# A new order of work in the second stage, on all four compute engines

## The chip, the core and the metric

One core of a Trainium2 chip runs the whole kernel. The metric is device time in microseconds of that core; lower is better. The core has TensorE (PE: matmuls and turns, into eight banks of PSUM), VectorE (DVE), ScalarE (ACT), GpSimd (POOL) and SyncE (SP, which issues the DMAs). Each runs its own list of instructions in order, and they wait for each other on semaphores.

## The reference

Two layers work on x of 4 sequences x 512 tokens x 128 features. The first layer and the attention of the second are not touched. What matters here is the feed-forward part of the second layer, a stack of six (`DEPTH`) local transformers:

```python
for i in range(6):
    x = attn_layer(shift_tokens(x), Wqkv[i], q_scale[i], k_scale[i], Wo[i]) + x
    x = ffn_layer(shift_tokens(x), ln_g[i], ln_b[i], W1[i], b1[i], W2[i], b2[i]) + x
# attn_layer: qkv = x @ Wqkv (128 -> 3 x 1024); q, k, v: 16 heads of 64
#   q = l2norm(q) * q_scale;  k = l2norm(k) * k_scale;  rotary tables on both
#   softmax of 8 * q k' over windows of 32 queries x 64 keys;  out = (attn @ v) @ Wo
# ffn_layer: hg = layernorm(x) @ W1 + b1 (128 -> 2 x 341);  a, gate = split(hg)
#   (a * gelu(gate)) @ W2 + b2
# shift_tokens: the upper half of the features comes from the token before
```

## The kernel before

The stack is cut into batches (a layer and one of its 4 sequences: 24 in all) and each batch into four tiles of 128 tokens. A tile is worked on in three consecutive slots. In slot g the projections and rotations of tile g are made, tile g-1 has its queries and keys turned and its scores and first softmax part made, and tile g-2 gets its exponentials, values and output turn. `t` is the position of a slot in its batch, 0 to 3; I call them slot 0 to slot 3. `run_slots` (L401) calls one `slot` function per engine, and each of these is a list of calls written out by hand: this list alone sets the order on its engine. No planner is involved.

What a slot holds, by the names used below:

- TensorE: six projections of 128 x 512, each three matmuls (`project`, L950): Q0, Q1, K0, K1, V0, V1 (c = 0 to 5), alternately into the two banks of `pj`; the turn of the queries and that of the keys (`turn`, L962, four 128 x 128 turns into each bank of `tr`); the turn of the probabilities (`turn_probs`) and of the outputs (`turn_out`), also in `tr`; the scores in two halves into `sc` (`window_scores`, 64 small matmuls each) and the values in two halves into `oo` (`values`).
- VectorE: for each of Q0, Q1, K0, K1 a rotation (`rotate`, L1580: two products, one with the cosine and one with the sine table) and a length sum (`lengths`); two clamps; the first softmax part (`soft1`: maximum and subtraction), the sums of the exponentials (`soft2`), and the weighting of the outputs (`weighted`).
- ScalarE: a square of each of Q0 to K1 (`square`; the rotation waits for it and the next projection in that bank for the rotation), the exponentials, six copies out of `tr` before and two after (`take_qk_part`, `take_probs`, `take_out`), the mask written into `sc`, two copies of V (`copy_v`), and two inverse roots (`inverse_root`, L1959: Ln, then Exp).
- POOL: adds the two products of a rotation (L2141), refines the inverse root in four small steps, and scales the rotated rows (L2155), once for the queries and once for the keys. `low_half` makes the small parts of the input rows.
- SP: eight or ten DMAs that lay the values out by windows (`windows`), and at a change of layer the new weights.

Beside this some slots hold work of the batches before (fillers). With m1 the batch before and m2 the one before that: slot 0 has the up projection of m2 in three chunks (`ff_up`), with `gelu` on ScalarE and `ff_gate` on VectorE; slot 1 the down projection (`ff_down`); slot 2 half 1 of the output projection of m1 (`wo_half`), then its norm: shifted input, entry turn (`norm_in`), statistics; slot 3 the norm's apply, return turn (`norm_back`) and end (`ln_finish`), and at its end half 0 of the output projection of the batch itself.

At a change of layer ScalarE rounds each new weight matrix to its high part (`weights_high`) and VectorE or POOL makes the low part (`weights_low`), K0, K1, V0 and V1 of the next layer wait for theirs. `log_exp_tables` (L1765) writes out a load of ScalarE's tables that serve Ln and Exp. Other loads are put in by the compiler where a function needs one; they show at the line of the activation (L1761).

Of the kernel before, what the change touches and what calls it, by code (L numbers as in the profile page):

```python
# [11 lines left out]
ALU = mybir.AluOpType  # L12
# [96 lines left out]
def build(nc, ins, out):  # L109
    ctx = ExitStack()  # L110
    with ctx:
# [251 lines left out]
        FFB = (sc, tr, oo)  # L363
        LD_W = (ld_q, ld_k, ld_v)
        LNB_BANKS = (oo[:, 0], oo[:, 1])
# [186 lines left out]
        def _(pe):  # L552
# [470 lines left out]
            def slot(s_):  # L1023
# [3 lines left out]
                tiles = g - 2 if new or b == 0 and t < 3 else NTILE  # L1027

                def values_(i):
                    if i == 0 and t == 0 and m1 is not None:  # L1030
                        pe.wait_ge(lnb_out, m1)
                        pe.wait_ge(y_att, m1 * 2 + 1)
                    if i == 0 and t == 1 and m2 is not None:
                        pe.wait_ge(ff_ev, m2 * FFC + 3)
                    if i == 0 and t == 3 and m1 is not None:
                        pe.wait_ge(lnb_norm, m1 + 1)
                    values(n2, g - 2, t2, i)

                def turn_probs_():
                    pe.wait_ge(e_exp, g - 1)  # L1040
                    for j in range(2):
                        if c_:
                            pe.wait_ge(qk_cp, g * 4 - 4 + j + 1)
                        else:
                            pe.wait_ge(o_cp, g * 2 - 6 + j + 1)
                        turn_probs(g - 2, j)

                def turn_q():
                    for j in range(2):
                        if g == 2:  # L1050
                            pe.wait_ge(qk_cp, 2 + j + 1)
                        wait(pe, o_cp, g * 2 - 6 + j + 1)
                        turn(g - 1, t - 1, j)

                def turn_k():
                    for j in range(2):
                        if d_:
                            pe.wait_ge(pt_cp, g * 2 - 4 + j + 1)
                        else:
                            pe.wait_ge(qk_cp, g * 4 - 4 + j + 1)  # L1060
                        turn(g - 1, t - 1, 2 + j)

                def out_():
                    for j in range(2):
                        if c_:
                            pe.wait_ge(qk_cp, g * 4 - 4 + 2 + j + 1)
                        else:
                            pe.wait_ge(pt_cp, g * 2 - 4 + j + 1)
                        if t == 0 and m2 is not None:
                            pe.wait_ge(ff_ev, m2 * FFC + 2)  # L1070
                        if t == 1 and j == 1 and m2 is not None:
                            pe.wait_ge(y_ff, m2 + 2)
                        turn_out(g - 2, j)

                def wo_half(m, i):
                    pe.wait_ge(o_cp, (m * T + 2 + 2 * i) * 2)
                    half = slice(i * (S // 2), (i + 1) * (S // 2))
                    for p_ in range(PAIRS):
                        last = mm((oo, sc)[i][:, 0, half], wo[:, p_, :], oT[:, p_, half], start=(p_ == 0),
                                  stop=(p_ == PAIRS - 1))  # L1080
                    if i == 1:
                        last = mm(sc[:, 0, 0:S // 2], w_hi[0][:, 0:P], xs_hi[:, 0:S // 2], start=False,
# [3 lines left out]
                def ff_down(m):  # L1086
                    for k, (o, w) in enumerate(CH):
                        pe.wait_ge(ff_ev, m * FFC + 3)
                        last = mm(tr[:, 1], w2[0:w, k, :], fa[0:w, k, :], start=(k == 0), stop=(k == FFC - 1))
                    last.then_inc(w2_mm, 1)  # L1090

                def value_part(c):
                    if new:
                        if b == 0 and t == 0 and c == 4:
                            pe.wait_ge(wl_ok[2], l + 1)
                        project(g, t, c)

                if new:
                    if b == 0 and t == 0:
                        pe.wait_ge(wl_ok[0], l + 1)  # L1100
                    if t < 2:
                        pe.wait_ge(xs_l, n * 2 + t + 1)
                    project(g, t, 0)
                    project(g, t, 1)
                if c_:
                    turn_q()
# [1112 lines left out]
```

## Time and profile before

| | |
|---|---|
| median of 3 runs | 2330.42 us (2330.19 to 2330.95) |
| the profiled execution | 2331.1 us, its span 2329.3 us |
| PE / DVE / ACT / POOL busy | 2055.0 / 1827.6 / 1499.3 / 1164.6 us |
| granted clock of TensorE, mean | 0.979; 1.00 in nearly all of the second stage |
| second stage (six layers) | from about 620 us to the end |

Busy shares are of the span. Matmuls overlap each other in the trace, so busy TensorE isn't TensorE at its peak; the start of one instruction to the start of the next is what it occupies.

### The profile page before, as it was taken

To read this page: it belongs to the slowest core of one execution; us is meant where nothing else is said; L and a number is where in the kernel's file an instruction comes from. 1 tells how busy PE (TensorE), PEld (TensorE's weight loads), DVE (VectorE), ACT (ScalarE), POOL (GpSimd) and SP (SyncE) were. 2 spreads that over 40 slices of the span, in tenths; PEclk is the share of its full clock that TensorE was granted. 3 is DMA by queue.
4 is the path that set the end of the run, shared out by engine and by line. 5 is a ranking of instruction groups with operands and counts; after the bars stand their busy time and mean duration, and the time that the engine had idled before them with its cause. 6 is when DMAs were issued, how large, how long until landed. Compare 5 with 4: busy or idle time off the path is not lost.

```text
span 2329.3 us, 82692 instructions
## 1 busy us (share of the span) xinstructions
PE 2055.0 (88%) x34492; PEld 1472.0 (63%) x34492; DVE 1827.6 (78%) x3797; ACT 1499.3 (64%) x2993; POOL 1164.6 (50%) x1373
## 2 busy tenths in 40 slices
PE   6888899887589999999999998999989999989996
PEld 4656654455367766667667666766666766666763
DVE  6778764578589888888887888888887888888883
ACT  4666653365266677676777667666676666767663
POOL 1111100000377666666666666666676666766660
PEclk9999999999699999999999999999999999999998
DMA  4000000000122222222322223322222322322221
GB/s 107 2 1 2 2 1 1 0 1 1 51 76 64 70 74 73 72 64 57 99 64 70 66 55 84 81 63 69 58 82 65 82 55 71 90 59 66 70 59 33
DMA packets 94677, 125.84 MB, mean 54 GB/s; under 512 B 27484, under 2 KB 42466, under 8 KB 94306
## 3 DMA queue, kind: packets, MB, share of 16 engines
q1 hardware_dynamic: 94306, 120.54, 19.7%
q8 instruction: 276, 4.52, 0.8%
q14 instruction: 95, 0.78, 0.1%
HBM read 21.91 MB, written 1.05 MB: 10 GB/s over the span
## 4 chain that ended last, share of the span: by engine, by line
PE 46%; DVE 13%; ACT 12%; issue 8%; POOL 2%; DMA 1%; SPq 0%; ACTq 0%; POOLq 0%; DVEq 0%
PE pj L554 12%; PE oo L554 10%; PE sc L554 10%; ACT arena L1761 9%; PE tr L557 9%; PE tr L554 5%; DVE arena L1592 2%; DVE arena L1590 2%; DVE xn L1209 1%; DVE arena L1611 1%; DVE arena L1613 1%; PE oo L557 1%; DVE stats L1197 1%; DVE arena L1622 1%; DVE arena L1598 1%
## 5 line engine op out<-in xcount | busy, mean ns | idle before, releaser
L1761 ACT ACTIVATE arena<-tr 128x512 f32<-128x512 f32 (+2 forms) x874 | 456.3, 570 | 144.6 <-PE tr L557 96.5
L2141 POOL TENSOR_TENSOR arena<-arena 128x1024 f32<-128x1024 f32 x192 | 456.5, 2377 | 159.8 <-DVE arena L1592 153.1
L1761 ACT ACTIVATE arena<-pj 128x512 f32<-128x512 f32 x576 | 338.9, 592 | 271.0 <-PE pj L554 269.9
L557 PE MATMUL tr<-ident,arena 128*128 128x128 f32 x2974 | 426.0, 278 | 66.2 <-ACT arena L1761 45.0
L1761 ACT ACTIVATE arena<-arena 128x16 f32<-128x16 f32 (+6 forms) x808 | 354.5, 452 | 125.0 <-DVE arena L1606 69.1
L557 PEld LDWEIGHTS tr<-ident,arena 128*128 128x128 f32 x2974 | 340.8, 141 | 147.7 <-issue 105.8
L2155 POOL TENSOR_TENSOR arena<-arena 128x1024 f32<-128x1024 f32 x192 | 365.6, 1904 | 27.8 <-POOL arena L2151 0.4
L1590 DVE TENSOR_TENSOR arena<-pj,rtab 128x512 f32<-128x512 f32 x384 | 259.8, 677 | 116.6 <-ACT arena L1761 112.5
L1592 DVE TENSOR_TENSOR arena<-pj,rtab 128x512 f32<-128x512 f32 x384 | 261.5, 681 | 0.0
L2109 POOL TENSOR_TENSOR rstd<-rstd,half_neg 128x4 f32<-128x4 f32 x40 | 40.6, 1016 | 438.6 <-DVE rstd L1204 438.6
L1598 DVE TENSOR_REDUCE arena<-arena 128x8 f32<-128x512 f32 x384 | 259.7, 676 | 0.0
L554 PE MATMUL oo<-slab,arena 64*32 64x64 f32 (+1 forms) x12416 | 229.8, 228 | 27.5 <-DVE xn L1209 13.2
L554 PE MATMUL pj<-w_lo,xs_hi 128*128 128x512 f32 x576 | 228.5, 397 | 0.0
L554 PEld LDWEIGHTS oo<-slab,arena 64*32 64x32 f32 (+1 forms) x12416 | 157.8, 106 | 111.7 <-issue 78.1
L1611 DVE TENSOR_REDUCE arena<-sc 128x16 f32<-128x1024 f32 x96 | 117.6, 1225 | 117.2 <-PE sc L554 116.8
L554 PEld LDWEIGHTS sc<-arena 64*32 64x32 f32 x12288 | 135.1, 105 | 95.9 <-issue 94.0
L554 PE MATMUL sc<-arena 64*32 64x64 f32 x12288 | 168.7, 224 | 9.9 <-issue 8.3
L1631 DVE TENSOR_TENSOR slab<-oo,arena 128x1024 f32<-128x1024 f32 x96 | 117.0, 1219 | 11.5 <-PE oo L554 10.1
L1377 DVE CUSTOM_DVE_ANT_0 arena<-pj,biases 128x128 f32<-128x128 f32 (+3 forms) x214 | 101.0, 486 | 28.9 <-PE pj L554 28.1
L1613 DVE TENSOR_TENSOR arena<-sc,arena 128x1024 f32<-128x1024 f32 x96 | 117.5, 1224 | 3.3
L2145 POOL TENSOR_TENSOR arena<-arena 128x16 f32<-128x16 f32 x192 | 45.4, 236 | 144.8 <-ACT arena L1761 144.7
L1622 DVE TENSOR_REDUCE arena<-arena 128x16 f32<-128x1024 f32 x96 | 116.0, 1209 | 0.0
(275 smaller groups left out, 3800.5 us busy)
## 6 DMA issues: line engine op xcount, KB each, us to landing
slab<-arena SPq DMA_DIRECT2D x576, 128.0 KB
slab<-arena SPq DMA_DIRECT2D x336, 64.0 KB
wqkv<-in_L_ffn_Wqkv SPq DMA_DIRECT2D x18, 512.0 KB, 3.8
wo<-in_L_ffn_Wo SPq DMA_DIRECT2D x6, 512.0 KB, 4.3
w<-in_L_ffn_W SPq DMA_DIRECT2D x6, 341.0 KB
YT<-in_L_attn_x SPq DMA_DIRECT2D x4, 256.0 KB, 3.9
arena<-in_L_ffn_W SPq DMA_DIRECT2D x1, 1024.0 KB
out_x<-arena SPq DMA_DIRECT2D x4, 256.0 KB, 2.3
```

The lines of the kernel that those rows point to most:

```text
L554: return nc.tensor.matmul(o, l, r, start=start, stop=stop, **k)
L557: return nc.tensor.transpose(o, i, ident[0:i.shape[0], 0:i.shape[0]])
L1590: v.tensor_tensor(ra[:, t % 2, k, co].rearrange("p (h u d) -> p h u d", u=2, d=DL // 2), src, tc_.unsqueeze(1).broadcast_to(wide), ALU.mult)
L1592: v.tensor_tensor(rb[:, k, co].rearrange("p (h u d) -> p h u d", u=2, d=DL // 2), src[:, :, ::-1, :], ts_.unsqueeze(1).broadcast_to(wide), ...
L1598: v.tensor_reduce(ss[:, k, hf * PAIRS:(hf + 1) * PAIRS, 0], sq[:, c % 2].rearrange("p (h d) -> p h d", d=DL), AX.X, ALU.add).then_inc(ss_o ...
L1611: v.tensor_reduce(mx, s_v, AX.X, ALU.max).then_inc(mx_ok, 1)
L1613: v.tensor_tensor(Tm.rearrange("p (a u) b -> p u a b", u=2), sc[:, :, :].rearrange("p u (a b) -> p u a b", b=2 * WIN), mx.rearrange("p (u ...
L1622: v.tensor_reduce(sm, Ex, AX.X, ALU.add).then_inc(sm_ok, 1)
L1631: v.tensor_tensor(On.rearrange("p (a u d) -> p u a d", u=2, d=DL), oo[:, :, :].rearrange("p u (a d) -> p u a d", d=DL), ri.rearrange("p (a ...
L1761: return nc.scalar.activation(o, i, f, **k)
L2141: p_.tensor_tensor(r_, r_, rb[:, k, :], ALU.add).then_inc(sum_ok, 1)
L2155: p_.tensor_tensor(r3, r3, rs[:, k, :].unsqueeze(2).broadcast_to([P, HL, DL]), ALU.mult).then_inc(qk_rdy, 1)
```

## The change

All of it lies in the second stage. No matmul, activation or vector operation is added or taken away. The slot lists of TensorE, VectorE, ScalarE and POOL are written anew, the same for all four positions. In short:

- Half 0 of the output projection moves from the end of slot 3 to slot 0 of the next batch, ahead of K0, and into another bank; both halves and the down projection now stand between the query turn and K0.
- Chunk 0 of the up projection goes to `oo` in place of `sc`, the down projection to `oo` in place of `tr`, the norm's return turn to `tr` in place of `oo`.
- The query turn stands behind chunk 0 and half 1 of the output projection; the probabilities behind K0; V0 behind the second half of the values.
- VectorE does both query rotations before the length sums, and both key rotations before the third one.
- ScalarE: the inverse roots stand late in the slot, behind V's copies, and the first of them between the GELUs of chunks 0 and 1; the copies of outputs are the last of the slot. The mask stands behind the fourth square.
- POOL makes both additions first and scales later.
- The low part of the key weights is made at the start of the layer instead of at the end of the one before.

```diff
-        FFB = (sc, tr, oo)
+        FFB = (oo, tr, oo)
+        WOB = (sc[:, 0], oo[:, 1])
-        LNB_BANKS = (oo[:, 0], oo[:, 1])
+        LNB_BANKS = (oo[:, 0], tr[:, 0])
```

The new order on TensorE (what is not in a new place is left out):

```diff
+                    queries(0)
+                    queries(1)
                 if t == 0 and m2 is not None:
+                    wait(pe, on_ok, weighted_)
                     pe.wait_ge(lnb_out, m2 + 1)
...
                     ff_up(m2, 0)
                 if t == 2 and m1 is not None:
+                    wait(pe, on_ok, weighted_)
                     wo_half(m1, 1)
+                if c_:
+                    turn_q()
+                if t == 0 and m1 is not None:
...
+                    pe.wait_ge(t_sub, g - 1)
+                    wo_half(m1, 0)
+                if t == 1 and m2 is not None:
+                    ff_down(m2)
...
                     project(g, t, 2)
                 if d_:
+                    probs()
+                if new:
+                    project(g, t, 3)
+                if d_:
                     values_(0)
                 if c_:
                     turn_k()
-                if t in (2, 3) and d_:
+                if d_:
                     values_(1)
+                if t == 3 and m1 is not None:
+                    if c_:
+                        pe.wait_ge(qk_cp, (g - 1) * 4 + 3)
...
+                    norm_back(LNB, LNB_BANKS[1], m1)
                 if new:
...
+                    project(g, t, 4)
+                if c_:
+                    window_scores(g - 1, (t - 1) % T, 0)
                 if t == 0 and m2 is not None:
...
                     ff_up(m2, 1)
+                if t == 2 and m1 is not None:
...
+                    norm_in(LNB, LNB_BANKS[0], xsF)
+                if new:
+                    project(g, t, 5)
                 if t == 0 and m2 is not None:
...
+                    pe.wait_ge(ff_ev, m2 * FFC + 1)
                     ff_up(m2, 2)
                 if c_:
                     window_scores(g - 1, (t - 1) % T, 1)
-                if t == 0 and d_:
+                if d_:
                     out_()
```

Waits that the new banks bring: the values of slot 0 wait for gate 0, those of slot 1 for the feed-forward sum, those of slot 2 for the second attention sum; the output turn of slot 3 waits for the end of the norm.

VectorE's new order: R0, R1, L0, [slot 0: gate 0], [slot 3: norm apply], L1, [slot 0: attention sum 0], [slot 1: feed-forward sum], [slot 2: attention sum 1], `soft2`, R2, clamp 0, R3, L2, `weighted`, [last batch of a layer, slot 0: tables], L3, clamp 1, [slot 0: gates 1, 2], [slot 2: norm statistics], `soft1` (R rotation, L length sum). Before, each L followed its R, gate 0 stood ahead of `weighted`, and gate 2 and the norm statistics stood behind `soft1`.

ScalarE:

```diff
+                if new:
+                    wait(ac, ss_ok, g * 4 - 1)
+                    square(g, 0)
+                    wait(ac, ss_ok, g * 4)
+                    square(g, 1)
...
+                    act(Ex, Tm, ACT.Exp, scale=8.0).then_inc(e_exp, 1)
+                if c_:
+                    take_qk_part(g - 1, (t - 1) % T, 0)
+                if t == 0 and m2 is not None:
+                    gelu(m2, 0)
+                if c_:
+                    take_qk_part(g - 1, (t - 1) % T, 1)
+                if new:
+                    ac.wait_ge(ss_ok, g * 4 + 1)
+                    square(g, 2)
...
+                    take_probs(g2, 0)
...
+                    take_probs(g2, 1)
...
+                    square(g, 3)
+                if layer_end:
+                    weights_high(l + 1, 0)
+                if t == 2 and m1 is not None:
...
+                    shifted(xsF, YT[:, s_.y1:s_.y1 + S], 0, S).then_inc(xs_f, 1)
+                if c_:
...
+                    mask(g - 1, (t - 1) % T)
+                    take_qk_part(g - 1, (t - 1) % T, 2)
+                    take_qk_part(g - 1, (t - 1) % T, 3)
...
+                    copy_v(g, t, 0)
+                if layer_end:
+                    weights_high(l + 1, 1)
...
+                    ln_finish(LNB, LNB_BANKS[1], m1, lcur[:, 0:1], lcur[:, 1:2], hB)
+                if new:
+                    inverse_root(g, 0)
+                if t == 0 and m2 is not None:
+                    gelu(m2, 1)
+                if new:
+                    copy_v(g, t, 1)
+                if t == 0 and m2 is not None:
+                    gelu(m2, 2)
+                    log_exp_tables()
+                if new:
+                    inverse_root(g, 1)
+                if d_:
...
                         take_out(g2, t2, j)
```

POOL:

```diff
+                if s_.new:
+                    add_parts(g, t, 0)
+                    if s_.ahead is not None and b == B - 1 and t == T - 1:
+                        weights_low(l + 1, 0)
+                    add_parts(g, t, 1)
+                    newton(g, 0)
+                    if t == 0:
+                        low_half(n * 2 + 2, YT[:, s_.y0:s_.y0 + S], P, S)
+                    scaled(g, t, 0)
+                    if s_.ahead is not None and t == 1:
+                        low_half(n * 2 + 3, YT[:, s_.ahead:s_.ahead + S], 0, P)
+                    newton(g, 1)
+                if t == 2 and s_.m1 is not None:
                     power(LNB, s_.m1)
                 if s_.new:
...
+                    scaled(g, t, 1)
```

## Rows read from the trace of the kernel before

**Rows 1.** The page: busy time and share per engine; the chain by engine.
```profile
PE 2055.0 (88%) x34492; PEld 1472.0 (63%) x34492; DVE 1827.6 (78%) x3797; ACT 1499.3 (64%) x2993; POOL 1164.6 (50%) x1373
...
PE 46%; DVE 13%; ACT 12%; issue 8%; POOL 2%; DMA 1%; SPq 0%; ACTq 0%; POOLq 0%; DVEq 0%
```

**Rows 2.** Windows, slots 0 to 3: stretch, length, busy by engine, clock, DMA, GB/s.
```profile
1505.61:1523.49 17.88, 17.18 (x320) 11.62 (x319) 13.42 (x22) 13.85 (x23) 10.01 (x10) 1.00 0.19 51
1523.49:1539.56 16.07, 14.60 (x313) 10.35 (x312) 13.15 (x21) 10.79 (x24) 10.45 (x13) 1.00 0.33 91
1539.56:1555.30 15.74, 15.74 (x329) 12.89 (x328) 13.49 (x21) 11.26 (x23) 9.95 (x11) 1.00 0.27 71
1555.30:1573.89 18.59, 16.04 (x327) 12.50 (x326) 18.32 (x39) 11.77 (x24) 14.26 (x21) 1.00 0.27 68
sum 68.28, PE 63.56 PEld 47.36 DVE 58.38 ACT 47.67 POOL 44.66; mean PE 15.89 PEld 11.84 DVE 14.60 ACT 11.92 POOL 11.16
```

**Rows 3.** Timeline, ACT, end of the norm, once a batch: start, duration, idle before.
```profile
1570.19 0.78 ACT L1761 ACTIVATE hT<-oo,lcur 128x512 f32<-128x512 f32 x1 [0.79 <-PE oo L557]
...
1639.20 0.78 ACT L1761 ACTIVATE hT<-oo,lcur 128x512 f32<-128x512 f32 x1 [1.29 <-PE oo L557]
...
1709.05 0.78 ACT L1761 ACTIVATE hT<-oo,lcur 128x512 f32<-128x512 f32 x1
...
1781.39 0.78 ACT L1761 ACTIVATE hT<-oo,lcur 128x512 f32<-128x512 f32 x1 [0.79 <-PE oo L557]
```

**Rows 4.** Waits of PE, 700 to 2280 us: total, times, longest.
```profile
PE tr L557 <- ACT arena L1761: 36.3, 45, 1.0
...
PE tr L554 <- ACT arena L1761: 14.9, 17, 1.6
```

**Rows 5.** Timeline, PE: chunk 0, down projection, output projection half 1.
```profile
1508.05 1.88 PE L554 MATMUL sc<-hT,w 128*128 128x512 f32 x4
...
1532.65 2.84 PE L554 MATMUL tr<-arena,w 128*128 128x512 f32 x6
...
1542.08 3.62 PE L554 MATMUL sc<-arena,wo 128*128 128x256 f32 x16
```

**Rows 6.** Timeline, DVE: a rotation, then the first softmax part.
```profile
1567.42 0.68 DVE L1590 TENSOR_TENSOR arena<-pj,rtab 128x512 f32<-128x512 f32 x1
1568.02 0.68 DVE L1592 TENSOR_TENSOR arena<-pj,rtab 128x512 f32<-128x512 f32 x1
...
1569.54 1.23 DVE L1611 TENSOR_REDUCE arena<-sc 128x16 f32<-128x1024 f32 x1
1570.80 1.23 DVE L1613 TENSOR_TENSOR arena<-sc,arena 128x1024 f32<-128x1024 f32 x1
```

**Rows 7.** Timeline, ACT: two copies of the query turn.
```profile
1558.17 1.09 ACT L1761 ACTIVATE arena<-tr 128x512 f32<-128x512 f32 x2
```

**Rows 8.** Timeline, ACT: loads of tables and what follows them.
```profile
1512.78 1.28 ACT L1761 ACT_TABLE_LOAD   x1
1514.07 0.69 ACT L1761 ACTIVATE arena<-sc,lcur 128x512 f32<-128x512 f32 x1
...
2310.85 1.28 ACT L1761 ACT_TABLE_LOAD   x1
2314.77 0.69 ACT L1761 ACTIVATE arena<-sc,lcur 128x512 f32<-128x512 f32 x1 [2.64 <-PE sc L554]
```

**Rows 9.** The page, costliest groups: additions and scalings on POOL.
```profile
L2141 POOL TENSOR_TENSOR arena<-arena 128x1024 f32<-128x1024 f32 x192 | 456.5, 2377 | 159.8 <-DVE arena L1592 153.1
...
L2155 POOL TENSOR_TENSOR arena<-arena 128x1024 f32<-128x1024 f32 x192 | 365.6, 1904 | 27.8 <-POOL arena L2151 0.4
```

**Rows 10.** Change of layer: SP and ACT timelines; the page's DMA issues, us to landing.
```profile
1700.38 9.63 SPq L477 DMA_DIRECT2D wqkv<-in_L_ffn_Wqkv  x3
...
1707.01 1.06 ACT L1761 ACTIVATE wk_hi<-wqkv 128x1024 fp32r<-128x1024 f32 x1 [0.50 <-DMA wqkv<-in_L_ffn_Wqkv]
...
wqkv<-in_L_ffn_Wqkv SPq DMA_DIRECT2D x18, 512.0 KB, 3.8
```

More of the change, by code:

```diff
@@ L1026, in slot, with queries @@
                 n2, t2 = (n, t - 2) if t >= 2 else (n - 1, t + 2)
[L1027 to L1046, printed above, removed]
+                weighted_ = min(g - 2, NTILE)
+                def queries(c):
+                    if c == 0 and t < 2:
+                        pe.wait_ge(xs_l, n * 2 + t + 1)
+                    project(g, t, c)
                 def turn_q():
                     for j in range(2):
-                        if g == 2:
-                            pe.wait_ge(qk_cp, 2 + j + 1)
-                        wait(pe, o_cp, g * 2 - 6 + j + 1)
+                        if g >= 3:
+                            pe.wait_ge(o_cp, (g - 3) * 2 + j + 1)
+                        elif g == 2:
+                            pe.wait_ge(qk_cp, 3 + j)
                         turn(g - 1, t - 1, j)
@@ L1086, in ff_down @@
                 def ff_down(m):
+                    pe.wait_ge(ff_ev, m * FFC + 3)
                     for k, (o, w) in enumerate(CH):
-                        pe.wait_ge(ff_ev, m * FFC + 3)
-                        last = mm(tr[:, 1], w2[0:w, k, :], fa[0:w, k, :], start=(k == 0), stop=(k == FFC - 1))
+                        last = mm(oo[:, 0], w2[0:w, k, :], fa[0:w, k, :], start=(k == 0), stop=(k == FFC - 1))
                     last.then_inc(w2_mm, 1)
[L1092 to L1096, printed above, removed]
                 if new:
@@ L1719, in slot @@
                     ln_stats(LNB, LNB_BANKS[0], m1, m1)
-                if s_.ahead is not None and b == B - 1 and t == T - 1:
-                    weights_low(l + 1, 1)
+                if c_:
+                    soft1(g - 1)
             ve.sem_inc(y_ff, 1)
@@ L2000, in slot @@
                 g2, t2 = g - 2, (t - 2) % T
-                def out_():
+                layer_end = s_.ahead is not None and b == B - 1 and t == T - 1
+                if new:
[4 more added lines that the diff above has]
+                if d_:
+                    ac.wait_ge(t_sub, g - 1)
+                    wait(ac, e_tr, g2 * 2)
+                    wait(ac, sm_ok, g2)
+                    act(Ex, Tm, ACT.Exp, scale=8.0).then_inc(e_exp, 1)
@@ new lines, in slot @@
+                if c_:
+                    if t == 0 and m1 is not None:
+                        ac.wait_ge(y_att, m1 * 2 + 1)
+                    mask(g - 1, (t - 1) % T)
+                    take_qk_part(g - 1, (t - 1) % T, 2)
+                    take_qk_part(g - 1, (t - 1) % T, 3)
+                if new and t == 0:
+                    wait(ac, pj_mm, n * (6 * T))
+                    shifted(xs_hi, YT[:, s_.y0:s_.y0 + S], P, S).then_inc(xs_h, 1)
+                if new:
+                    wait(ac, o_mm, g - T + 2)
+                    copy_v(g, t, 0)
@@ L2062, in slot @@
-                if s_.ahead is not None and t == 3:
-                    if b == B - 1:
-                        table(g + 1, l + 1, 0)
-                        weights_high(l + 1, 0)
-                    if l > 0 or b == B - 1:
-                        ac.wait_ge(y_ff, n + 1 - B + 2)
-                    ac.wait_ge(pj_mm, n * (6 * T) + 6)
-                    shifted(xs_hi, YT[:, s_.ahead:s_.ahead + S], 0, P).then_inc(xs_h, 1)
-                if new:
-                    wait(ac, o_mm, g - T + 2)
-                    copy_v(g, t, 0)
@@ L2086, in slot @@
-                if s_.ahead is not None and b == B - 1 and t == 3:
+                if layer_end:
                     table(g + 1, l + 1, 1)
```

232 lines of the change are left out of this document (83 added, 149 removed).

## The prediction

> **What bounds the kernel now.** The page comes first: TensorE is busy for 88% of the span, VectorE for 78%, and the chain that ended last is 46% TensorE, 13% VectorE, 12% ScalarE [rows 1]. So TensorE paces and the other two hold it up now and then. Next come the windows of one batch, cut at the first query projection of each tile slot [rows 2]: 68.28 us for four slots, of which TensorE is busy for 63.56. The third slot (15.74 us) is full; the others stand with gaps. Third, the marker that recurs once a batch [rows 3]: 69.0 us inside a layer, 69.9 and 72.3 on the two sides of a change of layer. The row of 1639.20 less the one of 1570.19 is the higher of what plain batches show, 68.28 in the windows the lower; I take 68.6. The two at the change are together 5.0 us longer than two plain ones.
>
> Who keeps TensorE waiting is mostly ScalarE [rows 4]: the turn of the keys or outputs waits for a copy that frees its bank.
>
> **TensorE's floor.** The full slot holds one half of the output projection, 3.6 us [rows 5], the entry turn of the norm, 0.4 (half of a pair of turns), and about 0.3 of small holes. What every slot has is therefore 15.74 - 3.6 - 0.4 - 0.3 = 11.45. A feed-forward chunk is 1.88 less 0.15 of overlap with what follows, 1.73, the down projection 2.8 [rows 5]. A batch is 4 x 11.45 + 3 x 1.73 + 2.8 + 2 x 3.55 + 0.8 = 61.7, so waits cost 68.6 - 61.7 = 6.9. That is all an order can give.
>
> **What each part does to it.** No matmul, copy or vector instruction is added or taken away; they move. VectorE per tile: a half-width rotation is two instructions 0.60 apart, a length sum about the same, the first softmax part 1.26 + 1.2 [rows 6]; with weighting and sums (1.2 each) and small ones this is 12.6 in every slot, with 2.0 for gates in slot 0, 1.4 for the norm's statistics in slot 2, 1.3 for its apply in slot 3: 56.5 a batch, below 61.7. ScalarE: 1.09 for two copies, 0.49 to the next and 0.60 to the end [rows 7]; about 9.4 a slot.
>
> I go through the four slots with these durations, each engine in its new order, time 0 at the first query projection, 0.25 from a TensorE end to the engine that waits (the same allowance everywhere), 0.1 elsewhere.
>
> Slot 0 holds four fillers: chunks 0, 1, 2 and, moved here from the end of slot 3, half 0 of the output projection. TensorE has 11.45 + 5.2 + 3.5 = 20.2 of work; the fillers cover VectorE's late start (first softmax part to 2.2, rotations 2.2 to 4.6), so K0 at 8.5 finds all ready. On VectorE gate 0 stands behind the first length sum and waits for GELU 0 until 6.3; nobody needs what is behind it before 9. The end is another matter. ScalarE now has the first inverse root (Ln, Exp) between GELU 0 and GELU 1, where nothing but copies and squares stood. One load of tables stands before the first GELU [rows 8] and one, written out, after the last (line 1765); in the new order Ln needs one, Exp perhaps a further one if Ln's set doesn't hold it, and GELU 1 another. I take three more at 1.29 (bounds: two, 2.6 us, and three, 3.9 us; with a load hidden in idle time worth nothing). They can start ahead of the wait of the instruction behind: one began at 2310.85, though its GELU waited for TensorE to 2314.77 [rows 8]. ScalarE: V0's copy to 14.2, three loads and the root to 18.4, GELU 1 to 19.0, gate 1 on VectorE 19.2 to 19.8. The output turn waits for gate 1 (the bank) and starts at 19.9 instead of 19.4; slot 0 ends at 20.8. Now 0.6 is lost there; with one load fewer, nothing.
>
> Slot 1: 11.45 + 2.8. The down projection stands before K0 and covers the start; K0 at 5.1 finds rotation 0 done at 3.6. Probabilities: exp done at 3.8, copies of the query turn 4.3 and 4.7, both in time. The values wait for the feed-forward sum (VectorE to 6.7) and start at 7.5. No wait over 0.1: 14.3.
>
> Slot 2: 11.45 + 3.5 + 0.4. The second half of the output projection covers the start. The norm's input (1.28 on ScalarE) now stands ahead of the mask, so the scores wait for the third copy, 11.75 against 11.45: 0.3. Slot 15.6.
>
> Slot 3 has no filler ahead of K0. Squares at 0.95 and 1.65, VectorE's first softmax part ends at 1.9, rotation 0 at 3.05: K0 at 3.2 against 2.25, wait 0.95. The apply of the norm ends at 6.15 and the values wait for it, 5.6 to 6.25: 0.65. The norm's return turn now needs the third copy (its bank is tr 0): 0.2. V0 waits for rotation 2: 0.2. 11.45 + 0.4 + 2.0 = 13.9, less 0.2 where waits overlap the pipeline: 13.7.
>
> Sum 20.8 + 14.3 + 15.6 + 13.7 = 64.4. I add 0.5 for what such a walk overlooks (nearest rows: the small holes in the full slot), 64.9, with bounds of 62.3 (floor plus 0.6) and 68.6.
>
> POOL gets two adds first and the two scalings last; per slot 2 x 2.38 + 2 x 1.90 [rows 9] and the small steps, 11 us, under every slot. Scaled queries are ready about 2.3 into the next slot, keys about 6.2; the query turn stands at 1.4 (slot 3: ready at 0.9), 3.2 (slot 0) and 4.9 (slot 2), in slot 1 at 1.5. All but hidden. What SP issues doesn't change in content or place among its own.
>
> **Change of layer.** In the last slot of a layer SP still issues the value windows first, then the weights; ScalarE found the key weights late, by 0.50, at 1707.01 [rows 10], 14 us into its slot. The rounding of the query weights now stands before the mask. By the new order the windows go out at -0.9 to 5.4, the query weights are issued at 5.4 to 6.0 and land 3.8 later [rows 10], 9.2 to 9.9; mask, key copies, return turn and all behind are 3.5 late. The slot is 17.2 instead of 13.7. VectorE's rounding of the key weights goes to the start of the next slot, beside fillers: nothing. So 3.5 to 4.5 for a change against 5.0 now: I take 4.5; the gain there, 0.5 x 5 = 2.5, I leave out against start and drain.
>
> **Sum.** (68.6 - 64.9) x 23 = 85. 23 are the 24 batches less one for the fill, where there are no fillers yet. The profiled execution took 2331.1 (span 2329.3, 1.8 around it) and stands 0.7 above the median of the runs. 2331.1 - 85 = 2246.
>
> The three loads and the skill: after a load the next instruction starts at once, 1512.78 to 1514.07 [rows 8], so a switch is 1.29. The Trainium skill, "ScalarE: Activation LUTs", section "What ACT_TABLE_LOAD costs", counts a drain as well and gives 2.66 us in all, and its section "Table sets: the hidden batching unit" says to batch calls by set; this change does the reverse. By its figure slot 0 would be some 4 us longer and the kernel about as fast as now.
>
> **Rivals.**
> (A) The forecast, 2225 to 2270: 50%.
> (B) Half the gain: small waits I don't see take 1.9 of the 3.7 a batch (each slot has some eight places at which one engine is let go by another within 0.5 us of being needed). 2331 - 43 = 2288: 23%. Against it: in slots 0 to 2 the fillers stand where the lags are.
> (C) All but the floor: 62.3, 6.3 x 23 = 145, 2186: 8%. For it: only two loads, or the waits of slot 3 shortened by slack carried over. Against it: slot 3 has no filler.
> (D) The other side: ScalarE paces the border of slots. It ends a slot with the second root and two copies of outputs, then two squares, exp, two copies, 5.5 us in a row before the probabilities. Each us it is late there comes four times a batch; it decides from 3.7 / 4 = 0.9 us on. The longest wait that TensorE shows on it today is 1.6 [rows 4]; with 1.3 at each border 4 x 1.3 - 3.7 = 1.5 a batch, +35: 2366. Against it: the out turn ends 0.6 before these copies have to be there. 9%.
> (E) The switches of tables cost double (2.6 each in place of 1.29): ScalarE's end of slot 0 moves 3 x 1.3 = 3.9, all of it on the path, 23 x 3.9 = 90 back: 2336. The row speaks against it. 5%. That is where the skill's figure would lead.
> (F) The order binds at other places and the loss equals the gain, within 0.2%: 5%.
>
> **Range and chances.** A, B and the near part of C: 2205 to 2312. 0.2% (4.7 us) is about what a measurement of this kernel tells from none. Faster is A, B, C: 81%, and a bit of the others: 0.83. Same: F and part of E, 0.05. Slower: D and the rest of E, 0.12.
>
> **What would show it.** Windows of a batch after: slots near 20.8, 14.3, 15.6, 13.7. Five table loads a batch instead of two, the middle three between V0's copy and GELU 1, and in slot 0 the only sizable TensorE wait ahead of the output turn, on gate 1. In slot 3 waits ahead of K0 (on the rotation) and the values (on the apply). In the last slot of a layer ScalarE idle on the load of weights ahead of the mask. TensorE busy near 92 to 95% in the second stage. Wrong it is if TensorE waits over 0.9 us at each border on ScalarE, or if slot 0 is over 23 us.

## The result, and the profile after

The changed kernel takes 2301.45 us (2299.22 to 2306.31, four runs), the kernel before beside it 2330.31 (2327.36 to 2330.95): a ratio of 0.9881 [0.9863, 0.9900], a small gain but clear of noise. Its profiled execution took 2299.22 us with a span of 2297.4. Against the 2331.1 of before that is 31.9 us gained where the prediction said 85. The sign is right and the time is inside the range, but over half of the gain, 53 us, is missing.

The page of the kernel after: busy time and share of each engine; the DMA queue that the page calls "instruction" (packets, MB, share of 16 DMA engines); the chain that ended last.

```profile
PE 2045.1 (89%) x34492; PEld 1478.3 (64%) x34492; DVE 1842.3 (80%) x3791; ACT 1607.4 (70%) x3059; POOL 1153.7 (50%) x1373
...
q8 instruction: 276, 4.52, 0.8%
...
PE 59%; DVE 8%; issue 6%; ACT 6%; POOL 1%; DMA 0%; POOLq 0%; ACTq 0%; DVEq 0%
```

Beside [rows 1]: the matmuls are the same in number. TensorE's share of the chain rose from 46 to 59%, and ScalarE's and VectorE's fell from 12 and 13% to 6 and 8%: the waits the change was to remove did go. VectorE's busy time rose by 15 us though it lost six instructions; cause 2 below alone adds 31.7 to it.

Windows of the kernel after, slots 0 to 3 of the batch that answers to [rows 2], in the same columns:

```profile
1488.46:1509.48 21.02, 20.28 (x338) 14.56 (x337) 14.38 (x23) 18.40 (x28) 12.79 (x16) 1.00 0.20 53
1509.48:1523.89 14.41, 14.38 (x315) 10.33 (x314) 13.88 (x22) 11.86 (x27) 9.66 (x12) 1.00 0.38 101
1523.89:1540.59 16.70, 15.69 (x329) 12.69 (x328) 14.86 (x29) 11.53 (x23) 12.71 (x16) 1.00 0.26 68
1540.59:1554.98 14.39, 12.40 (x313) 9.71 (x312) 14.29 (x25) 10.89 (x22) 9.14 (x11) 1.00 0.30 74
```

Predicted were 20.8, 14.3, 15.6 and 13.7. Slots 0 and 1 are as said within 0.2. Slot 2 is 16.70 here and 15.52 in batches without the stall that is shown under cause 1. Slot 3 is 0.7 too long. Without the stall the four make 65.3, against 64.4 in the prediction's walk.

The marker of the norm's end, as in [rows 3] (ScalarE, start and duration), over one change of layer:

```profile
1552.32 0.77 ACT L1761 ACTIVATE hT<-tr,lcur 128x512 f32<-128x512 f32 x1
...
1619.77 0.78 ACT L1761 ACTIVATE hT<-tr,lcur 128x512 f32<-128x512 f32 x1
...
1693.24 0.77 ACT L1761 ACTIVATE hT<-tr,lcur 128x512 f32<-128x512 f32 x1
...
1759.26 0.78 ACT L1761 ACTIVATE hT<-tr,lcur 128x512 f32<-128x512 f32 x1
```

In [rows 3] the change of layer stands on both sides of the third row, 1709.05. The row that answers to it here is 1693.24, so the two intervals at the change are 73.47 and 66.02; 67.45 is a plain one, as are the two ahead of the first row, 66.66 and 66.80. One change is a poor sample, for each holds its own share of stalls. Over the 22 intervals of the stage, 12 plain ones and five changes of two each:

| | after | before |
|---|---|---|
| a plain batch, mean | 67.6 us | 68.8 us |
| a change: its two intervals less two plain ones, mean | 2.2 us | 3.1 us |
| predicted: plain batch, change | 64.9, 4.5 | 68.6, 5.0 |

The gain is 1.2 x 23 = 27 us in plain batches and 0.9 x 5 = 5 at the changes, together the 32 that were measured. The prediction had 3.7 x 23 = 85 in plain batches and left the changes out. So what is missing is missing in the plain batch of the order after, which is 2.7 us longer than said.

**Cause 1, seen first in the waits of TensorE.** Kernel after, 700 to 2250 us (what TensorE waited for: total, times, longest), then the two lines of before that [rows 4] did not show (700 to 2280):

```profile
PE oo L555 <- issue: 22.7, 24, 2.2
PE tr L558 <- issue: 17.6, 24, 1.5
...
PE sc L555 <- issue: 10.3, 18, 1.2
```

```profile
PE sc L554 <- issue: 7.8, 11, 1.5
PE oo L554 <- issue: 6.7, 14, 1.5
```

"Issue" is a wait for nothing that the profile shows. The second of the three such lines of after is plain at a closer look: the output turn waits for gate 1 on VectorE, as predicted (below). The lines of oo and sc are something else. They fall in the middle of a group of 64 small matmuls whose inputs are long there, once or twice a batch. TensorE in slot 2 of the same batch:

```profile
1533.87 0.45 PE L555 MATMUL oo<-slab,arena 64*32 64x64 f32 x31
1535.23 0.48 PE L555 MATMUL oo<-slab,arena 64*32 64x64 f32 x33 [0.91 <-issue]
```

31 of the matmuls run, then 0.91 us of nothing, then the other 33. With the small lines (0.5 for pj after; 1.4 for the output turn's oo and 1.0 for pj before) these waits are 33.5 us after and 16.9 before. Sixty-four matmuls with 64 weight loads, 128 instructions in under 0.8 us, are the densest stretch of the program. The queue of instructions moves 4.52 MB in 276 packets, 16.4 KB each. It looks as if TensorE runs dry of instructions there; experiments 5 and 6 test that.

The packets themselves bear it out. The one DMA packet from 1532 to 1536 us, around the stall above, is of that queue (packets, MB, share):

```profile
q8 instruction: 1, 0.02, 1.4%
```

It starts at 1532.87 and ends at 1533.79, and TensorE goes on at 1535.23, 1.44 us behind its end. Read so from the trace, the order after has 39 stalls of 0.15 us or more inside groups of small matmuls (700 to 2230 us, 30.6 us in sum), and every one ends 1.2 to 1.6 us behind the end of a packet of this queue, though its packets come only every 6.6 us on average. In the order before it is the same for all 23 (13.5 us). So what it waits for is the next block of instructions.

Long waits can cost twice, whatever made them. A window of 3 us in the last slot of a layer (same columns; the 0.60 is the granted clock), and TensorE in and ahead of it:

```profile
1689.00:1692.00 3.00, 3.00 (x79) 2.16 (x80) 2.00 (x3) 0.20 (x1) 2.40 (x2) 0.60 0.02 5
```

```profile
1688.91 0.42 PE L555 MATMUL oo<-slab,arena 64*32 64x64 f32 x23 [2.07 <-issue]
...
1690.35 0.63 PE L555 MATMUL pj<-w_lo,xs_hi 128*128 128x512 f32 x1
```

Behind a wait of 2.07 us the granted clock is 0.60 on average, the lower level (1.2 GHz) for most of the stretch, and a projection matmul takes 0.63 where it takes 0.40 at the full clock. From 700 to 2230 us there are six such stretches of 3.4 us after and one before (behind a wait of 1.5). But only two of the six stand behind an issue wait, of 2.2 and 2.1 us. The other four stand behind a wait of 1.9 us for VectorE's rotation, which is cause 2. One of them:

```profile
998.77 0.50 PE L555 MATMUL pj<-wk_hi,xs_hi 128*128 128x512 f32 x1 [1.95 <-DVE arena L1595]
```

```profile
1000.10:1003.50 3.40, 3.40 (x73) 2.48 (x72) 3.40 (x7) 2.67 (x5) 2.26 (x1) 0.50 0.11 24
```

Nor does each such wait bring one: K0 waited 1.95 at 796.1 and 1952.6 us too, and the clock stayed full. By 0.63 for 0.40 a stretch costs about 1.2 us, and 1.7 at most (an estimate), so five more of them cost 6 to 9 us.

**Cause 2, in slot 3.** VectorE and POOL at the end of slot 2, and the first key projection (K0) of slot 3, kernel after:

```profile
1539.36 1.56 DVE L1207 TENSOR_SCALAR rstd<-mv 128x4 f32<-128x4 f32 x1
1540.83 1.21 DVE L1614 TENSOR_REDUCE arena<-sc 128x16 f32<-128x1024 f32 x1
```

```profile
1538.99 1.90 POOL L2154 TENSOR_TENSOR arena<-arena 128x1024 f32<-128x1024 f32 x1
```

```profile
1544.55 0.50 PE L555 MATMUL pj<-wk_hi,xs_hi 128*128 128x512 f32 x1 [1.44 <-DVE arena L1595]
```

The addition of epsilon to four variances per partition takes 1.56 us and ends when POOL's scaling ends (1538.99 + 1.90 = 1540.89). Before it took 0.17 on average. It now stands where POOL scales the queries. The first softmax part starts behind it, the rotation is late, and K0 waits for it 1.44 us here and 1.6 on average (38.8 us, 24 times); 0.95 was predicted without that hold. The Trainium skill, "SBUF — State Buffer", section "Who interferes with whom", describes such a hold: VectorE in a two-port mode, which its `tensor_scalar` can enter, and GpSimd exclude each other for a whole instruction. The trace agrees (1.56 us for 128x4).

The group of these additions from 700 to 2250 us, after and then before (count, busy, mean ns, idle before):

```profile
L1207 DVE TENSOR_SCALAR rstd<-mv 128x4 f32<-128x4 f32 x23 | 35.4, 1541 | 0.8
```

```profile
L1204 DVE TENSOR_SCALAR rstd<-mv 128x4 f32<-128x4 f32 x22 | 3.7, 170 | 0.8
```

**The switches of tables.** ScalarE in slot 0 of the kernel after, then gate 1 and the output turn behind it:

```profile
1502.74 1.28 ACT L1761 ACT_TABLE_LOAD   x1
1504.03 0.22 ACT L1761 ACTIVATE arena<-arena 128x16 f32<-128x16 f32 x1
1504.27 1.28 ACT L1761 ACT_TABLE_LOAD   x1
1505.56 0.22 ACT L1761 ACTIVATE arena<-arena 128x16 f32<-128x16 f32 x1
1505.80 1.28 ACT L1761 ACT_TABLE_LOAD   x1
1507.09 0.69 ACT L1761 ACTIVATE arena<-tr,lcur 128x512 f32<-128x512 f32 x1
```

```profile
1507.81 0.75 DVE L1661 SCALAR_TENSOR_TENSOR arena<-tr,lcur,arena 128x512 f32<-128x512 f32 x1 [4.51 <-ACT arena L1761]
```

```profile
1508.66 1.06 PE L558 MATMUL tr<-ident,slab 128*128 128x128 f32 x8 [0.74 <-issue]
```

Three loads, 1.29 from start to start, as forecast; the turn starts 0.1 behind the end of gate 1 and loses 0.74 where 0.6 was forecast.

### The profile page after: what moved, and what is told of

It is laid out like the page before. It is cut to its first block, busy times and chain, and to the rows that moved or that the text cites. A ratio compares the mean times of both kernels' runs of the same rounds, so it can differ in the third digit from the quotient of the medians.

```text
span 2297.4 us, 82677 instructions
## 1 busy us (share of the span) xinstructions
PE 2045.1 (89%) x34492; PEld 1478.3 (64%) x34492; DVE 1842.3 (80%) x3791; ACT 1607.4 (70%) x3059; POOL 1153.7 (50%) x1373
## 3 DMA queue, kind: packets, MB, share of 16 engines
q8 instruction: 276, 4.52, 0.8%
## 4 chain that ended last, share of the span: by engine, by line
PE 59%; DVE 8%; issue 6%; ACT 6%; POOL 1%; DMA 0%; POOLq 0%; ACTq 0%; DVEq 0%
PE pj L555 16%; PE oo L555 16%; PE tr L558 13%; PE sc L555 11%; ACT arena L1761 3%; PE tr L555 2%; DVE arena L1593 1%; DVE arena L1595 1%; DVE xn L1212 1%; PE oo L558 1%; ACT sc L1761 1%; ACT xcur L1761 1%; DVE arena L1601 1%; ACT L1761 0%; DVE stats L1200 0%
## 5 line engine op out<-in xcount | busy, mean ns | idle before, releaser
L1761 ACT ACTIVATE arena<-tr 128x512 f32<-128x512 f32 (+2 forms) x874 | 461.3, 570 | 159.1 <-PE tr L558 110.4
L558 PE MATMUL tr<-ident,arena 128*128 128x128 f32 x2974 | 429.3, 279 | 18.8 <-DMA beta<-in_L_attn_betas 9.3
L555 PE MATMUL sc<-arena 64*32 64x64 f32 x12288 | 174.2, 225 | 12.8 <-issue 10.3
L555 PE MATMUL pj<-wk_hi,xs_hi 128*128 128x512 f32 x192 | 98.9, 515 | 39.2 <-DVE arena L1595 39.2
L1634 DVE TENSOR_TENSOR slab<-oo,arena 128x1024 f32<-128x1024 f32 x96 | 117.1, 1220 | 16.9 <-PE oo L555 14.5
L558 PE MATMUL tr<-ident,slab 128*128 128x128 f32 x768 | 104.9, 279 | 21.5 <-issue 17.7
L555 PEld LDWEIGHTS pj<-w_lo,xs_hi 128*128 128x128 f32 x576 | 111.7, 194 | 14.8 <-issue 10.6
```

What stands on the lines that cost most here:

```text
L555: return nc.tensor.matmul(o, l, r, start=start, stop=stop, **k)
L558: return nc.tensor.transpose(o, i, ident[0:i.shape[0], 0:i.shape[0]])
L1634: v.tensor_tensor(On.rearrange("p (a u d) -> p u a d", u=2, d=DL), oo[:, :, :].rearrange("p u (a d) -> p u a d", d=DL), ri.rearrange("p (a ...
L1761: return nc.scalar.activation(o, i, f, **k)
```

## The experiments

All are edits of the kernel after unless it says "before". Each is named by its number and subject.

**1. One load for logarithm and exponential.** The loads of the root are chosen one by one, Ln's set first and then one for Exp; an explicit load of the set that holds both replaces the two.

```
+ if t == 0 and m2 is not None: log_exp_tables()
  inverse_root(g, 0)
```

> The changed kernel with the load of the Ln/Exp tables written out ahead of the first inverse root of slot 0, so that Ln and Exp share one load: four loads a batch instead of five. Theory (the three extra loads put gate 1 on the path at the end of slot 0, 0.74 us a batch): ScalarE reaches GELU 1 1.28 us earlier, slot 0 shrinks from 21.0 to 20.3, 12 to 18 us less than the 2301. Rival (that wait is only where another loss shows, the fetch of TensorE's instructions, and would return elsewhere): 2296 to 2303.

Measured 2277.83 us (2272.04 to 2284.43), 0.9770 [0.9745, 0.9795] of before, 24 less than the change alone. ScalarE in slot 0, timeline:

```profile
1498.00 1.28 ACT L1765 ACT_TABLE_LOAD   x1
...
1499.77 1.28 ACT L1761 ACT_TABLE_LOAD   x1
```

Two loads stand here instead of three, the wait on gate 1 is all but gone (17.6 us in the stage before, 1.7 now), and slot 0 is 20.24. The expectation said 12 to 18 less. The other 6 are not accounted for by any line: the runs of this kernel spread over 12 us, and the two profiled executions are only 14.8 apart.

**2. Both GELUs together.** Root 0 goes ahead of GELU 0, so that the two loads a batch of the order before come back (49 in the run, 115 in the kernel after).

```
  # in slot 0; ScalarE: inverse_root(g, 0) taken from behind gelu(m2, 0)
+ inverse_root(g, 0)                   # behind the two copies of take_qk_part(.., 1)
  gelu(m2, 0)
  # VectorE: clamp and gate taken from their places
  lengths(g, 1)
+ clamp(g, 0); ff_gate(m2, 0)
```

> The changed kernel with clamp 0 behind the second length sum, gate 0 behind it, and the first inverse root ahead of GELU 0 in slot 0: nothing but copies and squares between the GELUs, two loads a batch as in the kernel before. Theory of the loads: the output turn of slot 0 waits no more, slot 0 20.3, 15 to 20 us less than the 2301; ScalarE busy some 90 us less. Rival as for the run with one load fewer: 2296 to 2303. Should the later gate 0 hold the values up, slot 0 has a new wait of 0.5 or more at 9 to 10 us.

Measured 2288.27 (2286.75 to 2293.22), 0.9818 [0.9798, 0.9837], 13 less, where 15 to 20 was expected. Slot 0 is 20.24 as in experiment 1, so what the switches cost in that slot is the wait on gate 1: once that is gone, two further loads less do not shorten it. New waits of TensorE came, four of each kind in the stage (700 to 2240 us); they can account for the smaller gain. The first kind:

```profile
PE pj L555 <- DVE w_lo L1642: 4.1, 4, 1.0
```

The second is on gate 0 (L1661, 3.5 us). On VectorE gate 0 now comes later and the clamp earlier, and at the start of a layer the low parts of the weights (L1642) are made in line with them; that this is what makes the waits was not tested.

**3. The addition of epsilon on POOL.** In the stage's norm only.

```
- v.tensor_scalar(rstd[:, :], mv[:, :, 1], EPS, None, ALU.add)
+ p_.tensor_scalar(rstd[:, :], mv[:, :, 1], 1.0, EPS, ALU.mult, ALU.add)   # just ahead of POOL's power
```

> The changed kernel with the addition of epsilon in the stack's norm done by POOL just ahead of its power, not by VectorE. In the changed kernel that VectorE instruction takes 1.34 us (median) instead of 0.17 and ends with POOL's scaling; the first softmax part and rotation 0 of slot 3 stand behind it and TensorE waits 1.4 to 1.8 for that rotation. Theory (VectorE is held by POOL's instruction): slot 3's wait ahead of K0 falls to about 0.6, 15 to 22 us less than the 2301. Rival (the wait ahead of K0 comes from the second softmax part and the square, the long instruction runs in idle time): within 4 us of 2301.

Measured 2285.5 (2283.09 to 2292.22), 0.9807 [0.9785, 0.9828], 16 less. VectorE, POOL and TensorE at the border of slots 2 and 3:

```profile
1537.00 1.23 DVE L1615 TENSOR_REDUCE arena<-sc 128x16 f32<-128x1024 f32 x1 [0.89 <-PE sc L555]
```

```profile
1538.84 0.20 POOL L2106 TENSOR_SCALAR rstd<-mv 128x4 f32<-128x4 f32 x1
```

```profile
1540.78 0.50 PE L555 MATMUL pj<-wk_hi,xs_hi 128*128 128x512 f32 x1 [0.59 <-DVE arena L1596]
```

The softmax part now waits only for its scores, K0 waits 0.59 to 0.61, and slot 3 is 13.52 where 13.7 was predicted. Slot 0 keeps its 0.74. The "issue" waits of oo grew to 33.0 (24 times, longest 3.7) from 22.7, and they are 31 to 33 in both other versions with this edit (experiments 4 and 8): a part of what one mends is taken there.

**4. Experiments 2 and 3 together.**

> Both edits, GELUs together and epsilon on POOL. If they add up: 32 to 40 us less than the 2301, about 2264. If the fetch of TensorE's instructions takes back what waits give (it catches up in every wait), half of it: 2280 to 2285.

Measured 2273.22 (2268.02 to 2280.07, five runs), 0.9753 [0.9730, 0.9776], 28 less; slots 20.24, 14.20, 16.44, 13.53. The two gains, 13 and 16, add up within the spread of the runs; the expectation had larger ones to add.

**5. Are the issue waits made by the window transfers?** These are nearly all that the DMA engines move in the stage beside instructions and weights. They are cut to 4 of 512 columns, in both kernels, so the result is another.

```
- f = slice(u * S, (u + 1) * S)
+ f = slice(u * S, u * S + 4)          # and 0:4 at each destination
```

> The changed kernel with every value-window DMA cut to 4 of its 512 columns (the same number of DMAs and semaphores, nearly no data; the windows of the values are left out). It asks what the waits called issue are that TensorE has in the middle of its groups of small matmuls (33 us in the second stage after, 17 before). Theory R (rate: the groups use up their instructions faster than they are fetched, wherever other DMAs stand): the waits stay, 28 to 36 us, time within 6 us of 2301. Theory C (the fetch queues behind the window DMAs): they fall under 12 us and the time by 20 or more.

> The same cut in the kernel before (the windows of the values are left out). Theory R: issue waits stay near 17 us, time within 5 us of 2331. Theory C: they fall under 6, time 8 to 12 lower.

Measured 2296.61 (2292.11 to 2298.74) for the order after, 0.9845 [0.9825, 0.9864], and 2326.65 (2322.78 to 2329.33) for the order before, 0.9980 [0.9970, 0.9991]: 5 and 4 us less. Waits of TensorE in the first, 700 to 2230 us:

```profile
PE oo L555 <- issue: 24.8, 24, 2.3
PE sc L555 <- issue: 5.4, 12, 1.0
```

30 us of issue waits remain without the traffic, where 33.5 stood with it; in the order before 11.6 remain of some 16 (one profiled execution each). So contention with the windows isn't what makes them; a small part may be theirs.

**6. Or by the density of instructions?** Half of the small matmuls of each group of scores and values is left out (so the result is another), and four matmuls of 256 columns stand in their place on TensorE. Both kernels, scores and values alike.

```
- for w in range(G):                     # 64 small matmuls a half
+ for w in range(0, G, 2):               # 32
...
+ for k_ in range(4):
+     last = mm(sc[:, 0, 0:2 * P], ident[:, :].bitcast(BF16)[:, 0:P], ident[:, :].bitcast(BF16), start=False, ...)
```

> The changed kernel with 32 instead of 64 small matmuls in each half of scores and values (two of four windows left out) and four matmuls of 256 bf16 columns behind them, so that a half takes about as long as before (0.4 + 4 x 0.11 = 0.83 against 0.79) with 72 instead of 128 instructions. Theory R: issue waits fall from 33 us to under 8, the time by 15 to 30 (up to 12 us of that can go into the slightly longer halves; compare with the same edit in the kernel before). Theory C: they stay over 25.

> The same edit in the kernel before. Theory R: issue waits fall from 17 us to under 4, time 5 to 15 lower than 2331; the distance between the two kernels then grows from 30 to 40 or 50 us. Theory C: the distance stays 30.

Measured 2297.36 (2295.22 to 2301.49), 0.9852 [0.9832, 0.9872], and for the order before 2359.70 (2359.47 to 2360.96), 1.0119 [1.0102, 1.0136]. The page of the order after, and TensorE's waits from 700 to 2230 us (left out: 7.1 and 0.3 on ScalarE):

```profile
PE 2087.3 (91%) x23740; PEld 1515.2 (66%) x23740; DVE 1831.9 (80%) x3791; ACT 1607.1 (70%) x3059; POOL 1152.9 (50%) x1373
...
q8 instruction: 192, 3.15, 0.6%
```

```profile
PE pj L555 <- DVE arena L1601: 32.3, 23, 1.4
PE oo L555 <- DVE xn L1218: 14.3, 23, 0.9
PE tr L558 <- issue: 8.1, 22, 0.7
```

No issue wait of oo or sc is left in either kernel, and from 700 to 2230 us no stretch at half clock. 10,752 fewer matmuls and as many fewer weight loads make 1.37 MB less of instructions: 64 bytes each, so a packet of 16.4 KB is 256 of them, two dense groups, 1.6 us. (The Trainium skill, "Advanced Engine Details and Errata", section "ISA Cache", says the same of a line, 16 KB for 256 instructions; the packets agree.)

A sparse group takes 0.95 or 1.03 us from its start to the start of what follows, where a dense one takes 0.79 and 0.83 was expected; it is so in both kernels. That cost hides the gain in each run by itself: after is 4 us lower where 15 to 30 was expected, before 29 higher where 5 to 15 lower was. Only the distance of the two orders can be read, and it has grown more than the 40 or 50 us expected: 2359.70 - 2297.36 = 62.3 us without the issue waits, 29 with them. The windows of one batch are 67.34 after and 70.15 before, 2.8 apart; in the dense kernels the plain batches are 1.2 apart. So without these waits the new order would gain 33 us more, of the 53 missing. Counted in the two traces, the difference is 33.5 - 16.9 = 16.6 us of issue waits and 6 to 9 us of half clock, 23 to 25 together (four of the half-clock stretches belong to cause 2); the other 8 to 10 were not taken apart, and other waits changed in these runs as well.

**7. Where does the gain come from?** The down projection goes behind the probabilities, so K0 of slot 1 has no filler ahead. (In the order before it stood later still, ahead of the first scores.)

```
- if t == 1 and m2 is not None: ff_down(m2)
  project(g, t, 2)                       # K0
  probs()
+ if t == 1 and m2 is not None: ff_down(m2)
```

> The changed kernel with the down projection of slot 1 behind the turn of the probabilities instead of ahead of K0. Theory (the gain comes from fillers that cover VectorE's lag at the border of slots): slot 1 then stands like slot 3, K0 waits 1 to 1.5 us for rotation 0 and the probabilities some tenths for the exponentials; slot 1 15.5 to 16 instead of 14.4, 20 to 35 us more than the 2301. Rival (order within a slot doesn't matter as long as TensorE has work, and the gain is from one place, such as the projection half moved): within 5 us of 2301.

Measured 2338.04 (2334.71 to 2341.75 in six runs; a seventh took 3617.68 and is left out of the reading), 1.0030 [1.0018, 1.0041], 37 more than the change alone, just over the 20 to 35 expected. K0 of slot 1:

```profile
1532.77 0.50 PE L555 MATMUL pj<-wk_hi,xs_hi 128*128 128x512 f32 x1 [1.25 <-DVE arena L1595]
```

The wait comes back in every batch, and slot 1 is 16.1 us or more (16.5 in the batch of this row) for 14.4. The 37 us are 1.6 a batch: this wait and later ones behind it. One filler in the wrong place takes back the whole gain of the change.

**8. Experiments 1 and 3 together, the best version.**

> The changed kernel with both single edits that gave most: the written-out load ahead of the first inverse root in slot 0, and epsilon on POOL. Slots 20.2, 14.3, 15.5 and 13.5 plus fetch waits as now. If they add up, 24 + 16 less than 2301: 2261. If the fetch of instructions takes part of it back: 2268 to 2275, like the kernel with the GELUs together and epsilon on POOL (2273).

Measured 2267.45 us (2264.95 to 2268.83, five runs), 0.9727 [0.9714, 0.9740]: 63 less than before and 34 less than the change. Windows of the slots (same columns) and waits, 700 to 2230:

```profile
1475.21:1495.46 20.25, 20.25 (x338) 14.57 (x337) 14.57 (x24) 17.41 (x27) 13.27 (x16) 1.00 0.23 60
...
1509.67:1526.93 17.26, 15.69 (x330) 12.68 (x328) 14.31 (x29) 11.52 (x23) 12.98 (x17) 1.00 0.27 69
1526.93:1540.45 13.52, 12.44 (x313) 9.63 (x312) 13.42 (x24) 10.75 (x22) 9.06 (x11) 1.00 0.29 74
```

```profile
PE oo L555 <- issue: 32.7, 25, 3.4
...
PE sc L555 <- issue: 8.2, 17, 1.5
```

Slot 0 is full to the last 0.01 us, as slot 1 (14.21) is, slot 3 is at 13.52, and slot 2 would be 15.7 but for two issue waits of 1.18 and 0.39. The single gains, 24 and 16, would make 40; 34 came, while the issue waits rose from 33 to 41. The expectations were 2261 if the gains add up and 2268 to 2275 if the fetch takes part of it back; the result is between them.

**9. The second key projection (K1) between the halves of the values.** In the version of experiment 8, to part two dense groups.

```
  probs()
- if new: project(g, t, 3)
  values_(0)
  turn_k()
+ if new: project(g, t, 3)
  values_(1)
```

> The kernel of the run before this one (one load, epsilon on POOL) with K1 moved from ahead of the values to between the key turn and the second half of the values, which sets the groups of small matmuls further apart. Theory R (fetch rate, the distance of groups counts): issue waits of the second stage fall from about 40 us to 20 to 30, and the time by 5 to 15. Against it stands the later square of K1, and rotation 3 and V1 behind it: if that binds, V1 shows waits of 0.5 or more for the rotation, and the time is 5 to 20 higher.

Measured 2412.88 (2410.24 to 2414.34), 1.0350 [1.0336, 1.0364], 145 more: a miss. Two of TensorE's waits and one ScalarE row:

```profile
PE sc L555 <- ACT arena L1762: 55.8, 60, 1.9
...
PE oo L555 <- issue: 25.9, 59, 1.3
```

```profile
1543.64 0.60 ACT L1762 ACTIVATE arena<-pj 128x512 f32<-128x512 f32 x1 [2.50 <-PE pj L555]
```

ScalarE's order was left as it was: it stands idle 2.50 us on the square of the projection that now comes later, and its mask and copies behind it are late for the scores. On top of that the clock fell to the lower level 15 times from 700 to 2230 us, for 3.4 us each, mostly behind these new waits. The issue waits did change as was hoped: stalls inside the dense groups fell from 41 (40.5 us) to 25 (15.1 us), each still 1.2 to 1.6 us behind a packet. The rest of the line of oo stands at the start of groups and is another kind. But whether the distance of the groups did that, or the new waits that give the fetch time, this run can't tell. So the remedy is not shown; moving a matmul alone, without the same move on ScalarE, costs far more than the issue waits.

## Why the prediction came out at half the gain

- **The walk of slots 0 to 2: right.** 20.8, 14.3, 15.6 said, 21.02, 14.41, 15.52 measured where no issue wait falls in. Experiment 7 shows for slot 1 that the filler ahead of K0 makes the gain, as the walk had it. (VectorE's 56.5 us a batch is 55.1 by its own terms, 4 x 12.6 + 4.7; nothing hangs on it.)
- **Three loads in slot 0, 0.6 on gate 1: right** (0.74). Experiment 1 confirms the other half of the step, "with one load fewer, nothing". The rival of doubled switches falls; the Trainium skill's 2.66 us for a switch, "ScalarE: Activation LUTs", "What ACT_TABLE_LOAD costs", isn't what these rows show (1.29).
- **"I add 0.5 for what such a walk overlooks": the step that failed.** It was sized by the small holes of one full slot, in a batch window chosen by chance with only 0.3 us of issue waits in it. The 7.8 and 6.7 us of issue waits stood in the waits of before and were not read. In the order after they are 33.5 us, 1.45 a batch: the allowance was a third of that, and the half clock behind long waits comes on top. They doubled as the waits for other engines went. That such waits had given the supply of instructions time to catch up is an inference; it fits experiments 3, 4 and 8, where the issue waits grow again as other waits go. Experiment 6 puts the whole effect on the gain at 33 us. That is rival B by its time and its form (half the gain, by waits not seen), though not by its mechanism, which was to be engines letting each other go late.
- **Slot 3, "first softmax part ends at 1.9": off.** It ends at 2.7, for the addition of epsilon was costed among "small ones" and lies under POOL's scaling in the new order. The slot is 14.39 for 13.7. Experiment 3 puts it at 16 us: there the softmax part ends at 1.8 and the slot is 13.52, so its sum held. Part of that is luck, for K0 waits 0.59 and not 0.95.
- **"3.5 to 4.5 for a change": the last slot right, the sum too large.** The last slot of a layer was to be 17.2; the five are 15.8 to 18.8, 17.3 on average, and experiment 6, without the stalls, has them 1.5 to 2.5 longer than a plain slot 3 where 3.5 was said. The excess of a change is 2.2 for 4.5, and before 3.1 for 5.0: the 5.0 came from the one change of before that holds a stretch at half clock. These errors did not make the miss; the changes gave 5 us that the sum had left out.
- **Base 68.6: right.** Plain batches of before are 68.8. But it held before's own issue waits (16.9 us, 0.7 a batch), and subtracting from it a walk without such waits counted them as gained.
- **Together:** the plain batch of after is 2.7 over 64.9. Issue waits beyond the allowance are 0.95 of it, half clock 0.3 to 0.45, slot 3 0.7, slots 0 and 1 0.3. About 0.4 stays open.
- **Rival D** (ScalarE at the border) is not seen: the two lines of TensorE's waits on ScalarE in the stage come to 1.4 and 0.3 us, where [rows 4] has 36.3 and 14.9.

## What to carry to other kernels

When waits for other engines are taken out of a pacing engine, ask first what feeds it: read its "issue" waits in the trace of before, and set an allowance from their total, not from a clean window. The same holds for a rare event such as a change of layer: average all of them, for one sample carries its own stalls. Before tiny instructions are moved, look up what the neighbour engine does at the new place; an addition on 128x4 cost 16 us of this kernel. And an explicit load of a common table set ahead of a Ln and Exp pair is a one-line gain (24 us here by the medians, 15 by the profiled executions) where a switch can't be avoided.

## What was not expected of the hardware

- TensorE stalls inside dense groups of small matmuls, mostly 0.5 to 2 us at a time (3.7 at most) and once or twice a batch, with all inputs there. All 39 such stalls of the order after end 1.2 to 1.6 us behind a packet of the instruction queue. They come where 128 instructions run in 0.8 us; with 72 in 0.95 to 1.03 none is left.
- Behind a wait of TensorE of about 2 us, for instructions or for VectorE, the granted clock was at its lower level for 3.4 us, six times in the stage after; behind other waits as long it was not.
- VectorE's `tensor_scalar` on 128x4 takes 1.54 us on average (0.96 to 1.72, 23 times) when POOL has a 128x1024 instruction running, and 0.17 otherwise; on POOL itself it takes 0.20.
